# Cross-attention on one core: the product with values moved in front of the scores

## What is computed

```python
def proj(t, W, b):
    t = t.transpose(0, 2, 1) @ W.T + b
    return t.reshape(N, nc, CHUNK, H, Dh)
qh, kh, vh = proj(q, Wq, bq), proj(k, Wk, bk), proj(v, Wv, bv)
scores = jnp.einsum('bnqhd,bnkhd->bnhqk', qh, kh) * scale
km = masks[:, 0, :].reshape(N, nc, CHUNK)
scores = scores + jnp.where(km[:, :, None, None, :] > 0, 0.0, NEG)
attn = jax.nn.softmax(scores, axis=-1)
out = jnp.einsum('bnhqk,bnkhd->bnqhd', attn, vh).reshape(N, T, C)
out = (out @ W_out.T + b_out).transpose(0, 2, 1) * masks
out = out + x
out = (out - mean(out, axis=2)) * rsqrt(var(out, axis=2) + EPS)
```

## Time and profile before

| What | us |
|---|---|
| Three runs | 2059.18 median, 2058.57 to 2062.14 |
| The profiled execution, time | 2053.5 |
| Its span on the chip | 2051.7 |
| PE busy | 1999.4 (97%) |
| DVE busy | 1682.0 (82%) |
| POOL busy | 1560.4 (76%) |
| ACT busy | 1487.3 (72%) |
| Chain of work that ended last, share of PE | 96% |

### The profile page before, as it was taken

How to read it: one execution, slowest core, us unless ns; L and a number is a source line. 1 busy time by engine, 2 the same in 40 slices (tenths; PEclk the granted TensorE clock), 3 DMA queues, 4 the chain that set the end, 5 groups by cost and what they waited for, 6 DMA issues and landing times.

```text
span 2051.7 us, 95454 instructions
## 1 busy us (share of the span) xinstructions
PE 1999.4 (97%) x42504; PEld 1633.8 (80%) x42504; DVE 1682.0 (82%) x2053; ACT 1487.3 (72%) x2177; POOL 1560.4 (76%) x1062
## 2 busy tenths in 40 slices
PE   6999999999999999999999999999999999999994
PEld 5888888888888888888888888888788887887883
DVE  4788888888888888888888888888888887888884
ACT  4677777777777777777777777777777777776774
POOL 4777777787777777777778787777777777877773
PEclk9999999999999999999999999999999999999996
DMA  4456666556656556656555665556665556655554
GB/s 155 116 151 175 171 180 182 166 155 176 180 170 171 173 165 177 182 172 169 161 168 172 188 180 161 158 172 177 172 176 168 161 171 173 179 164 154 163 152 129
DMA packets 242904, 342.81 MB, mean 167 GB/s; under 512 B 28992, under 2 KB 94784, under 8 KB 242496
## 3 DMA queue, kind: packets, MB, share of 16 engines
q1 hardware_dynamic: 242496, 336.71, 57.0%
HBM read 168.82 MB, written 67.11 MB: 115 GB/s over the span
## 4 chain that ended last, share of the span: by engine, by line
PE 96%; issue 1%; POOL 1%; ACT 1%; DVE 0%; DMA 0%; SPq 0%; POOLq 0%; ACTq 0%; DVEq 0%
PE proj_bank L291 37%; PE proj_bank L323 19%; PE proj_bank L345 18%; PE o_bank L392 10%; PE score_bank L368 9%; PE score_bank L361 3%; POOL y L554 0%; DMA ctx_raw<-ctx 0%; POOL ctx_lo L544 0%; ACT y L495 0%; POOL neg_rows L567 0%; ACT ctx_hi L427 0%; POOL prob L537 0%; POOL o_lo L576 0%; ACT q_f L466 0%
## 5 line engine op out<-in xcount | busy, mean ns | idle before, releaser
L537 POOL TENSOR_TENSOR prob<-prob,recip 128x1024 f32<-128x1024 f32 x256 | 487.8, 1905 | 329.4 <-DVE recip L627 327.2
L612 DVE TENSOR_REDUCE row_max<-score_bank 128x16 f32<-128x1024 f32 x256 | 313.4, 1224 | 298.9 <-PE score_bank L368 297.9
L435 ACT ACTIVATE prob<-prob 128x1024 f32<-128x1024 f32 x256 | 271.5, 1060 | 283.1 <-DVE prob L616 283.1
L544 POOL TENSOR_TENSOR ctx_lo<-ctx_raw,ctx_hi 128x512 fp32r<-128x512 f32 x256 | 331.0, 1293 | 48.8 <-ACT ctx_hi L427 48.5
L291 PE MATMUL proj_bank<-ctx_hi,w_hi 128*128 128x512 f32 x1024 | 349.0, 422 | 5.7 <-POOL ctx_lo L544 4.3
L554 POOL TENSOR_TENSOR y<-y,x_raw 128x512 f32<-128x512 f32 x256 | 325.4, 1293 | 4.6 <-DVE y L655 4.6
L616 DVE TENSOR_TENSOR prob<-score_bank,row_max 128x1024 f32<-128x1024 f32 x256 | 313.4, 1224 | 8.8
L291 PE MATMUL proj_bank<-ctx_hi,w_lo 128*128 128x512 f32 x1024 | 320.6, 394 | 0.0
L291 PE MATMUL proj_bank<-ctx_lo,w_hi 128*128 128x512 f32 x1024 | 318.0, 392 | 0.0
L635 DVE STREAM_TRANSPOSE squares<-prob 128x1024 f32<-128x1024 f32 x256 | 315.8, 1234 | 2.0 <-POOL prob L537 2.0
L623 DVE TENSOR_REDUCE sums<-prob 128x16 f32<-128x1024 f32 x256 | 304.7, 1190 | 1.2 <-ACT prob L435 1.1
(11 more groups left out here) (44 smaller groups left out, 3781.9 us busy)
## 6 DMA issues: line engine op xcount, KB each, us to landing
ctx_raw<-ctx SPq DMA_DIRECT2D x128, 512.0 KB, 5.8
x_raw<-x SPq DMA_DIRECT2D x128, 512.0 KB, 4.6
prob_t<-squares SPq DMA_DIRECT2D x1024, 64.0 KB, 2.5
out<-y SPq DMA_DIRECT2D x128, 512.0 KB, 6.0
mask_all<-mask SPq DMA_DIRECT2D x128, 256.0 KB, 4.2
v_x<-v_f SPq DMA_DIRECT2D x256, 128.0 KB, 3.5
y<-w_in_t SPq DMA_DIRECT2D x1, 768.0 KB, 4.4
y<-w_out_t SPq DMA_DIRECT2D x1, 256.0 KB, 4.4
```

Source lines behind the costliest of these rows:

```text
L537: pool.tensor_tensor(part, part, slots(recip[:, u % 2, :]), ALU.mult).then_inc(norm_done, 1)
L544: pool.tensor_tensor(ctx_lo[:, n % 2, :, tokens], ctx_raw[:, n % BLOCKS, :, tokens], ctx_hi[:, n % 2, :, tokens].bitcast(F32), ALU.subtrac ...
L612: dve.tensor_reduce(row_max[:, :].rearrange("p (r c) -> p r c", c=CPU), rows, AX_X, ALU.max).then_inc(max_done, 1)
```

## The change

In PE's `steps`, the call `probs_times_v(B, u - 2)` moves from between the two pairs of projections to the front of the step. No instruction is added, removed or altered, no semaphore changes its counts, and the queues of DVE, ACT, POOL and SP stay as they are.

```diff
             def steps(B):
                 for u in range(UNITS):
                     j, h = u // UPB, u % UPB
+                    probs_times_v(B, u - 2)
                     scores(B, u + 1)
+
                     for f in range(HALVES):
                         if h == 0:
                             project_out(B, j - 2, f)
                         else:
                             project_k(B, j + 2, f)
-                    probs_times_v(B, u - 2)
                     for f in range(HALVES):
                         if h == 0:
                             project_v(B, j + 1, f)
                         else:
                             project_q(B, j + 2, f)
```

## The result

| | before | after |
|---|---|---|
| Median of three runs, us | 2059.18 | 2363.44 (2355.2 to 2368.26) |
| Profiled execution, time and span | 2053.5, 2051.7 | 2355.2, 2353.4 |
| Ratio | 1 | 1.148, 95% interval 1.144 to 1.151 |

What follows compares the result with a forecast made beforehand. PE's queue was taken as the bound, busy 97% of the span. Two new waits over 126 pairs (197 us), unit 3 (20) and the clock (15) added 232 us, giving 2291 us, 11% slower, range 2235 to 2340.

Steps and rivals of the forecast that it cites:

- PE waits for `o_lo` in front of the even step: Product with values waits for DVE's L644; odd step 8.85 against 7.70 us, +1.15, and 0.62 more per batch at unit 3.
- the hand-over: From the end of DVE's `o_lo` to PE's start: 0.14 us, read from a wait at the tail.
- PE waits for `y`: In the even step `project_v` waits for DVE's L655 to free its bank; 8.23 against 7.82 us, +0.41.
- Values piece in front of masks: PE's product with values takes 0.79 us, then 1.09 from first mask to DVE's row maxima; piece bounds 0.6 and 0.99.
- The saving of unbroken projections: One break between PE's projections goes per step: at most about 0.2 us each, 52 us if nothing else binds.
- The clock: PE at half clock after half of unit 3's 32 waits, 0.9 us each: 15 us, bounds 0 and 43.
- The rival of half clock behind all waits: Half clock also follows PE's usual waits, adding 127 us: 2418 us; chance 10%, in part or in full.
- The part on waits that stay covered: Waits for `o_f` and copied keys stay hidden; POOL's and SP's queues are unchanged, and what hangs on earlier steps gains slack.
- Faster: Rival: five changes of shape become four and no wait appears, 2007 us; chance 2%.
- it cancels: Rival: one wait of half the size and the saving in both steps come out within 0.2% (4 us); chance 2%.
- only `o_lo` is real: Rival: DVE's L655 comes earlier, so the even step gains 0.2 in place of losing 0.41: 2214 us; chance 6%.
- theory B: From the experiments: besides the waits, adjoining small products use up PE's 256-instruction pages before the next is there.

Runs made afterwards that it cites:

- E4: Changed kernel with ACT's high_attention and copy_attention first in their step and DVE's low_attention first in its odd step, removing the `o_lo` wait: 2209.57 us, ratio 1.075.
- E7: Changed kernel with DVE's first output (`y`, half 0) put in front of the subtraction, so `project_v` need not wait: 2367.48 us, ratio 1.153.
- E1: Kernel before with the product with values moved directly behind the scores, ahead of the four projections: 2076.57 us, ratio 1.010.
- E5: Changed kernel with the product with values done for two of four chunks only from the second batch on, both waits kept: 2186.45 us, ratio 1.064.
- E3: Kernel before with the product with values moved to the front in even steps alone: 2276.61 us, ratio 1.103.

## Why the prediction was wrong, point by point

- **PE waits for `o_lo` in front of the even step: right.** 126 waits (forecast about 127), idle 1.22 in the pair shown (forecast 1.2), 33 of 126 over 2 us from start to start, 31 of them in unit 3's step (forecast 32). DVE's 6.83 held to the digit. The mis-sized term is the hand-over: 0.25 for 0.14. The tail row it was taken from is a wait inside one projection; here the first product of another shape and a chain of four semaphores follow; that these make the difference is not shown. E4 shows the size: without this wait, 154 us less.
- **PE waits for `y`: right.** 8.17 in an undisturbed even step, forecast 8.23. E7 shows that taking it away wins nothing here, as stops and half clock took back what the steps had gained.
- **Values piece in front of masks: right.** 1.91 from its start to the row maxima, forecast 0.79 + 1.09 = 1.88.
- **The saving of unbroken projections: right in size, and worth nothing.** E1's undisturbed batch is 1.3 us shorter than before, eight steps at 0.16.
- **The clock: right for its own cause.** E5, with hardly a stop, has 19 half-clock stretches (outside the tail), and 16 of them directly follow a long wait of unit 3; the forecast was 16. Its disturbance of 23 us stands against 15 forecast. The rival of half clock behind all waits did not come: in E5 the usual waits, 1.61 from start to start in the median, were followed by it only twice, and those two had lasted 1.7 and 1.9.
- **What failed: the sum's silence on "issue".** The sum has no term for PE running out of instructions, so it stood at nothing; the runs showed 60 us of such stops in place of 14, and with the half clock behind them 53 us that the forecast lacked. The part on waits that stay covered names queues and semaphores and asks of no one whether PE's own instructions arrive in time. The trace of before had the sign: the stop at 1718.54, which I read as a price of the clock and not as a thing that the change would multiply. It lies between two scores, at a 256th instruction.
- **The sum.** Profiled spans differ by 301.7 us, forecast 232. Of the 70 missing, the disturbance is (84 - 16) - 15 = 53, and the steps (69.15 - 68.94) x 31 = 7. Of the other 10, some 5 are the pair that the forecast started from: 4 x 15.52 = 62.08, where an undisturbed batch before took 61.90. The last 5 lie at the ends of the run (up to the seventh row maxima it took 2.1 longer, from the second last to the end 3.0).
- **The rivals.** None held. "Faster" and "it cancels" are out by the time, "only `o_lo` is real" by the 97 waits for `y`. The range was built from the bounds of the terms I had, and one term was not there. It wasn't even all of those: the upper bound of the product with values, 0.99, would have added 2 x 126 x 0.2 = 50 us. The measured time would then have lain inside, but by luck, since that piece took what was forecast.

**What stays open.** Why a fetch starts when it does. In none of the 3835 pages of the twelve traces did PE enter a page less than 2.16 us after the packet before it had started. So a stop comes in two ways. Either a page is used up fast: the median page ahead of a stop took 1.7 us in the changed kernel, and E3 has 16 pages under 2.5 us, all 16 with a stop. Or the packet starts late: the changed kernel's packets started 1.1 us after a page was entered (median of all), but ahead of the stops of the kernel before, whose pages took 4.4 us, it was 3.0 (median), up to 4.4. Late starts go with data transfers. In the changed kernel, where the DMA engines were over 80% busy with data in the first microsecond of a page (68 pages), the packet started 2.1 us into it (median); where they were 20 to 50% busy (160 pages), 1.1. At the longest stop it was 3.4 us, with the engines full. No run here changes the transfers, so whether they cause the long stops is not shown, and they may carry part of what theory B puts on density. How much of the disturbance is standing and how much half clock is also not separated.

## What to carry to other kernels

Before moving work to the front of an in-order queue, take the engine it waits for and add up the loop: from what starts that engine's step, through its last instruction, to the moved work and back. If that sum is over the present period, the difference is lost in each turn, however much slack the waits of the old order showed. And count instructions as well as microseconds: where an engine runs hundreds of tiny instructions in 2 us, ask whether they can be delivered, look for "issue" in the waits, and treat larger instructions between the small ones as cover that a tidier order takes away.

## What the hardware showed that I had not expected

- In 3835 pages of 256 PE instructions, none was entered less than 2.16 us after the 16.4 KB packet before it had started.
- PE can run out of instructions in the middle of a run of equal matmuls. Stops stood at every 256th instruction alone (35 of 36, 51 of 51, 58 of 58), after a 16.4 KB packet that had landed 1.3 us earlier, and lasted up to 4.3 us.
- A stop makes a second loss: half clock for 3.4 to 6.8 us behind many of them, in which twelve matmuls took 5.1 us in place of 2.96.
- A semaphore hand-over from DVE to PE took 0.25 us where PE's next product had another array shape and four waits, 0.14 inside a projection.
